# Two layers of edge messages on a graph: part of the sums written to memory as blocks of 112 neighbouring rows

## The reference: what is computed

```
h = max(layernorm(x), 0)
for l in 0, 1:
    m    = relu(h[src] + xe)                                    # one row for each edge
    mean = segment_sum(m, type*n + dst) / max(count, 1)         # for each type and node
    out  = einsum('rnd,rdo->no', mean, w[l]) + h @ root[l] + bias[l]
    h    = batch_norm(out)   (relu after layer 0)
result = x + h
```

## Time and profile before

| | us |
|---|---|
| median of 3 runs | 2535.77 |
| lowest, highest | 2532.77, 2540.87 |
| span of the profiled execution | 3011.2 |
| groups of layer 0 in it, PE's first product to POOL's last scatter | 125.6 to 1315.3 |
| groups of layer 1, POOL's first gather to its last scatter | 1499.6 to 2747.8 |

### The profile page before, as it was taken

The page is one execution under the profiler, slowest core; times in us unless marked ns, Lnnn a source line. Parts: engine busy times, 40 slices in busy tenths (PEclk is TensorE's granted clock), DMA queues, the critical chain, the costliest instruction groups (busy, mean ns, idle before and its releaser), DMA issues. The chain is left out here.

```text
span 3011.2 us, 50450 instructions
## 1 busy us (share of the span) xinstructions
PE 2477.2 (82%) x19096; PEld 2315.6 (77%) x19096; DVE 1916.1 (64%) x5063; ACT 969.3 (32%) x2076; POOL 1603.3 (53%) x1613
## 2 busy tenths in 40 slices
PE   2388888888888888889968888898988889887976
PEld 1387887888787887789857878787888878777965
DVE  7566776777766667748855555565665556554754
ACT  0233344444444444424311222222222222222555
POOL 7566555665556555520056666666666666663000
PEclk7699998988998999999978999899999999988986
DMA  9533433344433333359922222222222222224889
GB/s 348 197 102 116 137 127 128 128 129 133 133 128 127 128 118 122 113 208 418 371 66 67 63 84 62 85 65 85 65 86 64 85 64 84 78 73 176 312 320 403
DMA packets 241842, 436.67 MB, mean 145 GB/s; under 512 B 39075, under 2 KB 144126, under 8 KB 241596
## 3 DMA queue, kind: packets, MB, share of 16 engines
q1 hardware_dynamic: 166134, 237.95, 22.6%
q0 software_dynamic: 53808, 115.45, 12.5%
q10 hardware_dynamic: 21654, 79.99, 6.6%
HBM read 255.41 MB, written 177.83 MB: 144 GB/s over the span
## 5 line engine op out<-in xcount | busy, mean ns | idle before, releaser
L1481 PE MATMUL ps_y<-arena 128*128 128x128 f32 x11032 | 1517.4, 287 | 227.9 <-issue 200.7
L1481 PEld LDWEIGHTS ps_y<-arena 128*128 128x128 f32 x11032 | 1412.1, 202 | 303.5 <-issue 278.5
L770 POOL DMA_INDIRECT acc<-arena x788 | 776.3, 985 | 728.1 <-ACT arena L1294 448.4
L1078 DVE SCALAR_TENSOR_TENSOR arena<-ps_s,arena 128x512 f32<-128x512 f32 (+1 forms) x1386 | 842.7, 678 | 362.9 <-PE ps_y L1482 186.0
L759 POOL DMA_INDIRECT arena<-h_rows,arena x394 | 411.9, 1045 | 300.3 <-DMA h_rows<-chunk_mem 180.5
L1273 ACT ACTIVATE arena<-ps_y 128x512 f32<-128x512 f32 (+1 forms) x198 | 117.9, 595 | 1259.8 <-remote 953.3
L759 POOL DMA_INDIRECT arena<-in_x_dram,arena x394 | 397.9, 1010 | 126.6 <-issue 118.9
L1482 PE MATMUL ps_y<-arena 128*128 128x128 f32 x1576 | 324.1, 286 | 23.2 <-issue 22.3
L1493 PE MATMUL ps_o<-arena 128*128 128x128 f32 x1576 | 260.8, 303 | 51.6 <-issue 49.0
L1493 PEld LDWEIGHTS ps_o<-arena 128*128 128x128 f32 x1576 | 226.8, 213 | 74.4 <-issue 73.0
L1482 PEld LDWEIGHTS ps_y<-arena 128*128 128x128 f32 x1576 | 254.0, 201 | 29.3 <-issue 29.1
(11 more groups left out here) (230 smaller groups left out, 2251.7 us busy)
## 6 DMA issues: line engine op xcount, KB each, us to landing
arena<-in_edge_attr_dram SPq DMA_DIRECT2D x190, 256.0 KB
chunk_mem<-acc SPq DMA_DIRECT2D x55, 512.0 KB, 12.3
acc<-arena ACTq DMA_DIRECT2D x28, 896.0 KB
acc<-arena SPq DMA_DIRECT2D x28, 896.0 KB
arena<-in_x_dram SPq DMA_DIRECT2D x45, 512.0 KB, 9.8
arena<-acc SPq DMA_DIRECT2D x43, 512.0 KB, 10.1
chunk_mem<-hn_rows SPq DMA_DIRECT2D x41, 512.0 KB
out_dram<-arena ACTq DMA_DIRECT2D x38, 512.0 KB, 9.4
```

The lines of the kernel that those rows point to most:

```text
L770: pool.indirect_dma_start(out=acc[l], out_offset=at(idx_t[:, t:t + 1]), in_=ob[:, gg % OB, t // NG, :], in_offset=None, **how).then_inc(sc ...
L1078: ins = v.scalar_tensor_tensor(mk[:, m, r, 0:n], ps_type[gg % 2][:, 0:n], float(r), mt[:, gg % MT, 0:n], ALU.is_equal, ALU.mult)
L1481: te.matmul(ps_y[gg % 2][:, c], mk[:, gg % MKS[l], r, c], w_sb[l][:, r * D:(r + 1) * D], start=r == 0, stop=False)
```

## The change

Tiles 1 to 95 of the first stream, and 100 to 123, which are tiles 1 to 24 of the second, are no longer scattered by POOL. For these 119 tiles of each layer the sums are put in place of node: row k of the slot belongs to node (first node of the tile) + k, with zeros for nodes without an edge. SP then reads the first node of the tile into a register (`value_load` of `first_i`) and writes rows 1 to 112 of the slot by one ordinary DMA to 112 neighbouring rows of `acc[l]`. The block can reach over rows of the next tile, so the windows of a group wait until those of the groups before have landed (`wide_out`), and so does the scatter of the tile that follows a span. `sums_out` waits for the windows of group gg - 4 also. SP writes the windows of group n - 8 right after it has issued the edge rows of group n, and the last eight groups' after the loop. The flag is also set when a tile in a span reaches over more than 112 nodes.

DVE's setup gets operations for this: which tiles are wide (`is_wide`), how far they reach (`over`), the place of each row in its window (`near`), the first nodes (`first_i`).

```diff
@@ -113,6 +113,24 @@
...
+    WROWS = 112
+    SPANS = ((1, NG - 4), (NG + 1, NG + 24))
+    WIDE = [t for a, b in SPANS for t in range(a, b + 1)]
+    WB = WIDE[-1] // P + 1
+    assert all(a % NG > 0 and b % NG + 2 < NG and a // NG == b // NG for a, b in SPANS) and WROWS < P
+    def listed(g):
+        return [t for t in tiles(g) if t not in WIDE]
+    def in_window(g):
+        return [t for t in tiles(g) if t in WIDE]
+    def windows(gg):
+        return sum(len(in_window(k % NG)) for k in range(gg + 1))
     ORDER = [(g, t) for g in range(NG) for t in tiles(g)]
@@ -172,6 +190,13 @@
...
         goes_on = sb("goes_on", [P, NB])
+        is_wide = sb("is_wide", [P, WB])
+        behind = sb("behind", [P, WB])
+        over = sb("over", [P, WB])
+        most = sb("most", [P, 1])
+        near_end = sb("near_end", [1, len(SPANS)])
+        to_spare = sb("to_spare", [1, 1])
+        first_i = sb("first_i", [1, WB * P], I32)
@@ -451,6 +476,7 @@
...
         scat_out = [sem(f"scat_out{s}") for s in range(OB)]
+        wide_out = sem("wide_out")
         ve_ready = sem("ve_ready")
@@ -567,7 +593,7 @@
...
-            return sum(len(tiles(k % NG)) for k in range(gg % ring, gg + 1, ring))
+            return sum(len(listed(k % NG)) for k in range(gg % ring, gg + 1, ring))
@@ -652,10 +678,23 @@
...
+            def window_rows(g, l):
+                gg = l * NG + g
+                for t in in_window(g):
+                    sp.wait_ge(ob_ready, gg + 1)
+                    if gg > 0:
+                        wait(sp, wide_out, 16 * windows(gg - 1))
+                    first = sp.value_load(first_i[0:1, t:t + 1], min_val=0, max_val=P * (F + 1))
+                    sp.dma_start(acc[l][bass.ds(first, WROWS), :], ob[1:1 + WROWS, gg % OB, t // NG, :]).then_inc(wide_out, 16)
+            sp.wait_ge(idx_ready, 1)
             for l in range(L):
+                sp.wait_ge(acc_zero[l], 16 * ZN)
                 for n in range(NG):
...
                         edge_rows(n, l)
+                    if n >= 8:
+                        window_rows(n - 8, l)
@@ -681,6 +720,9 @@
...
                         table_dma(sp, own_at(i).rearrange("p (c d) -> p c d", d=D), h1_tab, OWN_FIRST[i], own_in[i % 2], True)
+                for g in range(NG - 8, NG):
+                    window_rows(g, l)
@@ -766,19 +808,25 @@
...
                     pool.wait_ge(tr_ps, gg + 5)
+                if not add and t in WIDE:
+                    return
+                if not add and t - 1 in WIDE:
+                    pool.wait_ge(wide_out, 16 * windows(gg - 1))
                 how = {"compute_op": ALU.add, "bounds_check": N - 1, "oob_is_err": False} if add else {}
                 pool.indirect_dma_start(out=acc[l], out_offset=at(idx_t[:, t:t + 1]), in_=ob[:, gg % OB, t // NG, :],
-                                        in_offset=None, **how).then_inc(scat_out[gg % OB], 16)
+                                        in_offset=None, **how).then_inc(counted if t in WIDE else scat_out[gg % OB], 16)
...
                 gg = l * NG + g
-                j = t // NG
-                if j > 0:
-                    pool.wait_ge(scat_out[gg % OB], 16 * (tiles_done(gg, OB) - len(tiles(g)) + j))
+                done = sum(1 for k in listed(g) if k < t)
+                if done > 0:
+                    pool.wait_ge(scat_out[gg % OB], 16 * (tiles_done(gg, OB) - len(listed(g)) + done))
                 elif gg > 0:
...
                 scatter(g, t, l, True)
+                if t in WIDE:
+                    pool.wait_ge(counted, 16 * (FE + l * len(WIDE) + sum(1 for _, k in ORDER[:ORDER.index((g, t)) + 1] if k in WIDE)))
@@ -790,6 +838,7 @@
...
                     pool.wait_ge(scat_out[s], 16 * tiles_done(last, OB))
+                pool.wait_ge(wide_out, 16 * windows((l + 1) * NG - 1))
                 pool.wait_ge(join_at_ready, 1)
@@ -874,8 +923,25 @@
...
                                             op0=ALU.subtract, op1=ALU.max, accum_out=falls[:, 0:1]))
+            t0 = spare_row[:, 0:WB, 0]
+            own.mark(v.tensor_scalar(is_wide[:, :], t0, float(SPARE_ROW + P * SPANS[0][0]), None, ALU.is_ge))
+            own.mark(v.tensor_tensor(over[:, :], dstf[:, 0:WB, T], dstf[:, 0:WB, 0], ALU.subtract))
+            for k, (a, b) in enumerate(SPANS):
+                if k > 0:
+                    own.link(v.tensor_scalar(behind[:, :], t0, float(SPARE_ROW + P * a), None, ALU.is_ge))
+                    own.link(v.tensor_tensor(is_wide[:, :], is_wide[:, :], behind[:, :], ALU.add))
+                own.link(v.tensor_scalar(behind[:, :], t0, float(SPARE_ROW + P * b), None, ALU.is_gt))
+                own.link(v.tensor_tensor(is_wide[:, :], is_wide[:, :], behind[:, :], ALU.subtract))
+            own.link(v.scalar_tensor_tensor(over[:, :], over[:, :], -float(WROWS), is_wide[:, :], ALU.add, ALU.mult))
+            for b in range(WB):
+                own.link(v.tensor_tensor(falls[:, :], falls[:, :], over[:, b:b + 1], ALU.max))
             own.link(v.tensor_scalar(falls[:, :], falls[:, :], 0.0, None, ALU.is_gt))
             dve.sem_inc(falls_ready, 1)
+            own.link(v.memset(behind[:, :], 1.0))
+            for a, b in SPANS:
+                own.link(v.scalar_tensor_tensor(behind[:, :], t0, float(SPARE_ROW + P * (b + 1)), behind[:, :],
+                                                ALU.not_equal, ALU.mult))
+            own.link(v.tensor_scalar(behind[:, :], behind[:, :], -1.0, 1.0, ALU.mult, ALU.add))
@@ -883,7 +949,8 @@
...
             own.mark(v.memset(agree[:, :, T:P], 0.0))
-            own.mark(v.memset(keep[:, :, 0:1], 0.0))
+            own.mark(v.memset(keep[:, WB:NB, 0:1], 0.0))
+            own.mark(v.tensor_tensor(keep[:, 0:WB, 0], keep[:, 0:WB, 0], behind[:, :], ALU.mult))
             own.join()
@@ -891,7 +958,16 @@
...
             own.link(v.tensor_tensor(keep[:, :, :], kill[:, :, :], keep[:, :, :], ALU.mult))
-            own.mark(v.tensor_tensor(kill[:, :, turned], keep[:, :, :], spare_row[:, :, :], ALU.add))
+            own.link(v.tensor_tensor(kill[:, :, turned], keep[:, :, :], spare_row[:, :, :], ALU.add))
+            near = keep[:, 0:WB, :]
+            own.mark(v.tensor_tensor(agree[:, 0:WB, :], dstf[:, 0:WB, 0:P], dstf[:, 0:WB, T:P].to_broadcast([P, WB, P]),
+                                     ALU.not_equal))
+            own.link(v.tensor_tensor(near, dstf[:, 0:WB, 0:P], dstf[:, 0:WB, 0:1].to_broadcast([P, WB, P]), ALU.subtract))
+            own.link(v.scalar_tensor_tensor(near, near, 1.0, agree[:, 0:WB, :], ALU.add, ALU.mult))
+            own.link(v.tensor_tensor(near, near, slot[:, 0:WB, :], ALU.subtract))
+            for b in range(WB):
+                own.link(v.scalar_tensor_tensor(slot[:, b, :], near[:, b, :], is_wide[:, b:b + 1], slot[:, b, :],
+                                                ALU.mult, ALU.add))
@@ -902,7 +978,18 @@
...
             dve.wait_ge(flag_ps, 1)
-            v.tensor_scalar(flag_i[:, :], ps_s[0][0:1, 0:1], 0.5, None, ALU.is_gt).then_inc(flag_ready, 1)
+            for k, (a, b) in enumerate(SPANS):
+                end = (b // NG + 1) * NG
+                own.link(v.tensor_tensor(near_end[:, k:k + 1], dst_t[0:1, end:end + 1], dst_t[0:1, b:b + 1], ALU.subtract))
+                own.link(v.tensor_scalar(near_end[:, k:k + 1], near_end[:, k:k + 1], float(WROWS), None, ALU.is_lt))
+            own.link(v.tensor_copy(most[0:1, :], ps_s[0][0:1, 0:1]))
+            for k in range(len(SPANS)):
+                own.link(v.tensor_tensor(most[0:1, :], most[0:1, :], near_end[:, k:k + 1], ALU.max))
+            own.mark(v.tensor_scalar(flag_i[:, :], most[0:1, :], 0.5, None, ALU.is_gt))
+            own.mark(v.tensor_scalar(to_spare[:, :], most[0:1, :], 0.5, float(SPARE_ROW), ALU.is_gt, ALU.mult))
+            own.join()
+            dve.sem_inc(flag_ready, 1)
+            own.link(v.tensor_scalar(first_i[:, :], dst_t[0:1, 0:WB * P], to_spare[:, 0:1], None, ALU.max))
             dve.wait_ge(cols_ps, 3)
@@ -1291,6 +1378,7 @@
...
                     act.wait_ge(scat_out[gg % OB], 16 * tiles_done(gg - OB, OB))
+                    wait(act, wide_out, 16 * windows(gg - OB))
                 a_.activation(ob[:, gg % OB, 0:w, :].rearrange("p w d -> p (w d)"), ps_o[gg % 2][:, 0:w * D],
...
```

## The result

| | before | after |
|---|---|---|
| median of the runs, us | 2535.8 (2532.77 to 2540.87) | 2360.55 (2359.04 to 2363.12) |
| ratio, 95% interval | | 0.9307 [0.9294, 0.932] |
| profiled execution's span, us | 3011.2 | 2361.3 |

The change saves 175 us. The changed kernel's profiled execution has the time of its other runs, unlike the one of before that the prediction was read from.

The account below looks back on a forecast made before the run. POOL's indirect DMAs were taken to set both layers' pace, 912 and 1044 us, giving 2550 us before. Less 38 + 83 = 121 us this is 2429, less 14 about 2415, put at 2420; range 2380 to 2535 us.

Parts of the forecast that it names:

- What bounds the kernel: Both layers: POOL's indirect DMAs set the pace in undisturbed runs, PE waits for slots; likeliest case, chance 0.76.
- the last step: Sign in the profile after: the profiled span hardly shortens, while the median falls by 4 to 5%.
- Layer 0: Layer 0's end moves from 1058 to 1016 us: gain 42 us, 38 after 4 us of setup.
- The losses of two nearly full engines: PE and DVE in layer 0 after the change wait for each other: 0.2 us a group, 20 us.
- the 912 us: Layer 0 before: POOL's 314 gathers and 394 scatters back to back from its first scatter at 146.2 us.
- Layer 1: Layer 1 takes 961 us after the change, against 1044 before: gain 83 us.
- The setup: DVE's added setup operations lengthen the chain to the first group by 4 us, counted in layer 0 alone.
- The windows: Register loads and windows on SP, 1.8 us each, cost nothing in layer 0; waits of following scatters taken as 0.
- Rival 1: PE is the bound without the profiler too, its gaps belong to the program: 2540 us, chance 0.13.
- Rival 2: SP becomes the bound in layer 1, stalling PE 9.1 us at each of 16 chunks: 2566 us, chance 0.09.
- Rival 3: A tile reaches over more than 112 nodes and the flag takes the fallback: 5510 us, chance 0.01.
- The 14 us that I took off: Excess of the sum for the kernel before over the median, subtracted from 2429 us: about 2415 us.

Follow-up runs that it names:

- experiment 2: Kernel before with the scatters of the 119 tiles left out in both layers and nothing in their place: 2359.99 us, ratio 0.9308.
- 3: Changed kernel, windows kept, with POOL again making the 119 scatters of each layer, into a table nothing reads: 2536.4 us, ratio 1.0003.
- experiment 7: Kernel before without the products of one of the 8 relations (outputs lack it): 2526.84 us, ratio 0.9971.
- e15: Changed kernel, unchanged, on a chip where the kernel before takes about 3000 us: 2718.74 us, ratio 0.9121.
- the first experiment: Kernel before, unchanged, run again for a second profile: 2529.52 us, profiled span 2527.7 us.
- e7b: Kernel before with the 119 scatters left out in layer 0 alone, on a chip of about 3000 us: ratio 0.9517.
- e12: Kernel before with the 119 scatters left out in layer 0 alone, repeated on a chip of about 3000 us: ratio 0.948.
- e13: Changed kernel with windows for the second stream's tiles 1 to 24 alone, on a chip of about 3000 us: ratio 0.9911 to the kernel before.
- e16: Kernel before with the 119 scatters left out in layer 0 alone, third time, on a chip of about 3000 us: ratio 0.9457.
- e8b: Kernel before with the scatters of tiles 1 to 30 left out in both layers, on a chip of about 3000 us: ratio 0.9751.
- experiment 6: Changed kernel without the products of one of the 8 relations (outputs lack it): 2294.34 us, against 2360.12 for the changed kernel.

## Why the prediction was right or wrong

**What bounds the kernel: right for the median, wrong on why the profile said otherwise.** Adding up POOL's instructions with the 0.305 us between them, against its 53% on the page, found the limit; experiments 2, 3, 7 and the waits of before bear it out. But I took PE's gaps for something of that one profiled execution. On three chips they are there in every run, and the last step, that the profiled span would hardly shorten, was wrong. It went from 3011.2 to 2361.3 us, since the second profile has none of the gaps. Where they are, too, the changed kernel's span (2733.9, e15) is 277 us shorter than that of the first profile, and its median 259 us shorter than that of before on the same chip.

**Layer 0, the step that failed: 38 us forecast, 86 measured.** The pace of 8.71 us a group was right, and POOL's end before PE's too. Two terms of the sum for the changed kernel were mis-sized, both to the same side. PE's start was taken from the first profile, 125.64 us, plus 4 for the setup, 129.6; it is 101.24, which is 28 us. I corrected the loop for the gaps of that profile and kept its start. The start is late by two long waits and not by gaps of 1 us: PE's second turn of a tile comes at 103.94 us where it is 91.03 in the first experiment, and the first product waits 19.73 us more for "remote", which stands in the very row that I took it from the earlier trace rows. Both waits come back in e7b, e12, e13 and e16, where the first product is at 124 to 126 us; what they are stays open. The losses of two nearly full engines, 0.2 us a group or 20 us, are next to none: from 101 to 963 us PE is busy for 859.6 of 862 us, beside a DVE with 817.3 us (98.5% of the window from 600 to 800 us). The drain is 5 us and not 8. 28 + 20 = 48 us, the whole difference of 86 and 38, with 3 us for the drain and 3.7 us for the end before, 1054.5 for 1058, against each other.

That the end before was right to 3.7 us is luck. POOL's first scatter was taken from the first profile as well, 146.2 us, where it is 122.0, 24 us too late. And the 912 us behind it are 932.5: the DMAs back to back are 915 (314 gathers, 394 scatters and 0.305 us between them hold), but the sum put POOL's waits in this stretch at nothing, and those for ACT and PE are 18 us. Late start and missing waits cancel. So the late start is in the sum for after with 28 us and in the sum for before with 4, and the difference is missing from the gain. The range missed the measured time because its low end of 2380 left out the losses but still had the late start in it. (Its upper term for layer 1 is a slip: 97 - 0.6 x 69 is 56, not 50 us.)

**Layer 1: 83 us forecast, 84 measured, with two errors that cancel.** After the change it was to take 961 us and takes 943 (without losses the sum was 947). Before it was to take 1044 us and takes 1027, since a gather takes 1.00 us there and not 1.049. I also miscounted: there are 22 chunks and 44 halves in groups 6 to 92, not 16 and 32 in groups 6 to 68, and SP had waited at 16 of them. The pace of 9.35 us a group up to group 92 comes from those 44 halves, where I had POOL at 9.2 from group 69, so the number hardly moved.

**The setup: 4 us, 1.4 measured** at the first product. In experiment 2, without it, the time is 0.6 us less. That is less than the difference of two runs. The size was right: PE's first turn of a tile starts at 92.67 us after and at 88.05 in the first experiment, 4.6 us later (the five operations on 128 columns, 0.27 us each in the sum without a row for it, take 0.28 to 0.35). What failed is that nothing covers them. PE had waited 6.75 us for `inv_rows` before its first product and now waits 2.56. On the other chips the first product comes at 124 to 127 us in the kernels without windows (e7b, e8b, e12, e16), at 126 to 157 us in those with windows for one stream and at 151 in the changed kernel (e15). So something in the setup with windows costs up to 30 us there, and why isn't shown.

**The windows: nothing, as forecast.** SP's register load takes 0.27 us, 0.44 with its two small followers, below the bounds of 0.5 and 1.4 us:

```profile
L687 SPq TENSOR_LOAD <-first_i x238: 262/268/475, 130.6 to 2075.8; - x119
...
L688 SPq DMA_DIRECT2D acc<-arena x238: 316/339/362, 131.5 to 2076.5; - x119
```

(duration in ns, min/median/max, and the first and last start). ACT waits 29.3 us in all for a scatter or window, 20 times, 3.0 at most, and PE's node sums stand idle for 3.8 us in the whole execution. One term was far off. POOL's scatters of tiles 96 and 124 were to wait 0 to 2.5 us for the windows of the group before, and I took 0:

```profile
POOL acc L816 <- DMA acc<-arena: 20.4, 1, 20.4
```

This is tile 124's scatter in layer 1. SP issues nothing from 1414.6 to 1436.2 us, where by its order it waits at a chunk for PE, and the windows of groups 23 and 24 come behind that chunk. So the scatter is made at 1444.56 us and not at about 1424. In the changed kernel it costs nothing, since POOL has time to spare and PE goes on (20.00 us busy from 1424 to 1444). In experiment 6 POOL has no such time.

**The rivals.** Rival 1, that PE's gaps are the limit and the time stays, is wrong on both kinds of chips: where there are none the gain is 175 us, and where there are, fewer scatters mean fewer of them. My own words on it, that 3011 us should then have been measured without the profiler, would on another chip have spoken for it. Rival 2, SP at the chunks, didn't come: DVE's longest wait for edge rows is 5.3 us, where it was 9.07. These waits do add up to more than in the first experiment, 93.8 us in 20 against 14.2 in 3, but experiment 2, which has no windows, has 92.7 us in 20, so they come with the faster groups. Of the 93.8 us 5.3 reach PE. The 20.4 us above are what SP's chunks did to a window. Rival 3 neither. The 14 us that I took off, as the excess of my sum over the median, were in truth 17 us too much for layer 1 and 4 for the end of layer 0, less some 6 us by which the first experiment's run lay under the median.

**The two rules that the prediction named.** Spreading DMAs saves only the issuing engine's time, says "DMA: Bandwidth & Descriptors" of the Trainium skill in "Rules for kernel authors". Experiments 2 and 3 agree, to 1 and 2 us. The change is worth 7% all the same, since that time was the limit. The rule of "Perfetto Trace Analysis" of the Trainium skill, section "Identifying the Most-Contended Engine", named TensorE for a kernel in which an eighth of its products by weights, left out, is worth 8 us in 2535 (experiment 7); here the measurement decides against it.

## What to carry to other kernels

An engine that issues DMAs is full when its instructions and the pauses between them add up to the stretch, whatever its busy share says; here 63% was full. When a profile stands far above the median of the runs, every number that rests on it has to be corrected, the start of the loop as well as its pace, and a wait that stands in the row itself is the place to begin; a profile whose time fits the runs is worth more than the correction. A loss for two engines that are nearly full belongs to the range, not to the sum, as long as no row shows one: here next to none came. And when a sum meets a measured time, check its start and its length apart: here the two were 24 and 20 us off and hid each other.
